# The first expert stage's opening slots moved into the drain of a lightning-attention stage, with routing in fewer slots

## The reference, cut to what matters

```
x = x + lightning_attention(layernorm(x))   # chunks of 128, 16 heads, a state carried from chunk to chunk
x = x + ffn(layernorm(x))                   # 32 experts of width 96, at most 7 of the top 8 in use per token
x = x + attention_b(layernorm(x))           # softmax attention with rotary positions
x = x + ffn(layernorm(x))                   # the same experts again

ffn:  probs = softmax(x @ gate_weight.T); top 8; keep those whose running share is under 0.8, plus one
      out  += (silu(g) * u) @ w_down.T * share        for each token and each expert kept for it
```

## Time and profile before

| | |
|---|---|
| median of 3 runs | 1141.58 us (1138.09 to 1143.42) |
| the profiled execution's own time | 1150.82 us |
| its span | 1149.0 us |
| PE busy | 893.2 us (78%) |
| POOL busy | 654.5 us (57%) |
| DVE busy | 586.1 us (51%) |
| ACT busy | 544.4 us (47%) |
| indirect DMAs issued by POOL | 288 results (995 ns each), 224 rows (1002 ns each) |
| mean granted TensorE clock | 0.894 |

### The profile page before, as it was taken

One profiled execution on the slowest core, in us unless ns is written; L12 is line 12 of the kernel. 1 busy time (PEld: TensorE's weight loads), 2 busy tenths in 40 slices (PEclk: granted clock), 3 DMA queues, 4 the chain that ended last, 5 costly groups with the idle time before them and its releaser, 6 DMA issues. The chain is left out here.

```text
span 1149.0 us, 20703 instructions
## 1 busy us (share of the span) xinstructions
PE 893.2 (78%) x5504; PEld 673.5 (59%) x5504; DVE 586.1 (51%) x2104; ACT 544.4 (47%) x1071; POOL 654.5 (57%) x652
## 2 busy tenths in 40 slices
PE   5999998852896699997338897988649877999940
PEld 4666665531785599996223453544228766999940
DVE  4566785845362122226846478664622711223565
ACT  5333456520463255654237767665515533555530
POOL 2576568776676777771541010474665567777760
PEclk9999999985798799999669898988878988999985
DMA  9900012122767777665230000125336587766976
GB/s 340 361 2 2 1 46 81 70 80 92 225 207 252 242 224 221 214 208 191 100 129 33 33 33 33 47 102 220 113 110 209 172 270 253 219 220 215 295 245 216
DMA packets 93231, 181.64 MB, mean 158 GB/s; under 512 B 18985, under 2 KB 73788, under 8 KB 92736
## 3 DMA queue, kind: packets, MB, share of 16 engines
q1 hardware_dynamic: 68544, 114.19, 31.1%
q0 software_dynamic: 24576, 66.13, 15.8%
HBM read 96.34 MB, written 92.27 MB: 164 GB/s over the span
## 5 line engine op out<-in xcount | busy, mean ns | idle before, releaser
L1295 POOL DMA_INDIRECT result_rows<-ys,result_slots x288 | 286.5, 995 | 105.5 <-issue 85.7
L981 POOL DMA_INDIRECT expert_rows<-route_rows,index x224 | 224.5, 1002 | 105.4 <-issue 91.0
L1944 ACT ACTIVATE b_probs<-ps 128x1024 f32<-128x1024 f32 x128 | 127.7, 1030 | 46.6 <-PE ps L1794 46.6
L1447 PE MATMUL ps<-w_gu,f_xts 128*128 x576 | 112.9, 341 | 3.1 <-issue 2.0
L1447 PE MATMUL ps<-w_gu,g_xts 128*128 x576 | 111.0, 337 | 3.8 <-ACT g_xts L1490 2.0
L1540 DVE SCALAR_TENSOR_TENSOR f_h<-ps,f_xs,f_gate 128x96 f32<-128x96 f32 x144 | 39.1, 313 | 121.0 <-ACT f_gate L1497 93.4
L1447 PEld LDWEIGHTS ps<-w_gu,f_xts 128*128 128x128 f32 x576 | 97.4, 199 | 5.6 <-issue 5.4
L1447 PEld LDWEIGHTS ps<-w_gu,g_xts 128*128 128x128 f32 x576 | 96.1, 197 | 6.2 <-issue 6.0
L1540 DVE SCALAR_TENSOR_TENSOR g_h<-ps,g_xs,g_gate 128x96 f32<-128x96 f32 x144 | 39.1, 313 | 115.2 <-ACT g_gate L1497 101.6
L1806 PE MATMUL ps<-b_probs,b_v_pad 128*32 128x512 f32 x512 | 78.3, 687 | 13.2 <-issue 6.9
L1508 ACT COPY ys<-ps 128x512 f32<-128x512 f32 x144 | 83.6, 581 | 1.8 <-PE ps L1466 1.8
(11 more groups left out here) (361 smaller groups left out, 1849.9 us busy)
## 6 DMA issues: line engine op xcount, KB each, us to landing
parts<-result_rows SPq DMA_DIRECT2D x32, 896.0 KB, 4.8
f_xs<-expert_rows SPq DMA_DIRECT2D x144, 160.0 KB
g_xs<-expert_rows SPq DMA_DIRECT2D x144, 160.0 KB
expert_rows<-pad_rows SPq DMA_DIRECT2D x64, 160.0 KB, 2.3
w_gu<-in_Wgu SPq DMA_DIRECT2D x1, 6144.0 KB, 17.5
expert_rows<-pad_rows SPq DMA_DIRECT2D x1, 5120.0 KB, 40.4
result_rows<-ys,result_slots POOLq DMA_INDIRECT x288, 3.4
f_w_d<-in_Wdown SPq DMA_DIRECT2D x1, 4096.0 KB, 29.8
```

Source lines behind the costliest of these rows:

```text
L981: self.nc.gpsimd.indirect_dma_start(xs, bass.IndirectOffsetOnAxis(self.index[:, f, t, r:r + 1].bitcast(U32), 0), self.x_rows(f)[:, t, :], ...
L1295: self.nc.gpsimd.indirect_dma_start(self.y_dram, bass.IndirectOffsetOnAxis(self.slots[:, i, j:j + 1].bitcast(U32), 0), self.ys[:, i, j, :] ...
L1447: ins = nc.tensor.matmul(ps[:, bank_gu[u % 2], j * GU:(j + 1) * GU], xts[:, u % 2, o:o + P], w_gu[:, k, bass.ds(experts[j] * GU, GU)], sta ...
L1944: nc.scalar.activation(probs[:, u % RING, :, :], ps[:, 2 * (u % 2):2 * (u % 2) + 2, :], ACT.Exp, scale=float(HD) ** -0.5).then_inc(exp_don ...
```

## The change

The experts are no longer a block of their own after lightning. `experts` becomes a set of generators, one for each engine, that yield after each slot. Lightning's block takes them as `then`: from unit 65 on (`THEN = DRAIN - THEN_SLOTS`) every drain unit ends with one slot of the experts on PE, ACT, POOL and DVE, so that slots 0 to 9 stand in units 65 to 74, and `run_all` appends the rest. SP starts them after its first loads and the last of lightning's projections. For the experts `g` after attention there is still a block of its own (`alone`). Their buffers (`Overlay`) lie over lightning buffers that are no longer read. In slots 0 to 9 of `f`, pairs have one PSUM bank for turned rows and one for gate and up in place of two (`Banks`), since the drain uses the others.

Routing's 15 steps stand in 11 slots (`TOGETHER`): 0 and 1 together, 3 (which is empty) left out, 9 with 11, 10 with 12. `PLACED` goes from 13 to 9, in lightning and in both expert stages. Batch 3's step 0 in `f` stands in slot 10. POOL's early result pairs, before batch 3's scatters, are 3 in place of 7 in both stages. A ring place of `xs` is given back at `h_ready`, when DVE has multiplied. The padding stores of `f` follow the load of pair 25 in one run; those of `g` start in slot 17; in both, four row numbers are loaded by one register load.

```
+THEN_SLOTS = 10
+    THEN = DRAIN - THEN_SLOTS
...
+            slots = then.tensor(pe)
             for u in range(UNITS, UNITS + DRAIN):
                 finish(u // QUADS, u % QUADS, B - 1)
                 route(UNITS * (B - 1) + u)
+                if u >= UNITS + THEN:
+                    advance(slots)
+            run_all(slots)
...
             first_loads(sp, 1)
+            sp.wait_ge(kv_sb, NT)
+            run_all(then.sync(sp))
...
-    STEPS = 15
-    PLACED = 13
+    TOGETHER = ((0, 1), (2,), (4,), (5,), (6,), (7,), (8,), (9, 11), (10, 12), (13,), (14,))
+    PLACED = len(TOGETHER) - 2
...
             if u >= RING:
-                sp.wait_ge(y_ready, u - RING + 1)
+                sp.wait_ge(h_ready, u - RING + 1)
...
-                if u >= 2:
-                    pe.wait_ge(h_ready, u - 1)
+            if banks.before(banks.gate_up, u) is not None:
+                pe.wait_ge(h_ready, banks.before(banks.gate_up, u) + 1)
...
+        def started(first, scattered):
+            return first + max((Routing.ALL - scattered) // 2, Routing.PLACED)
...
+        def results_at(u, first, scattered, last):
+            start = started(first, scattered)
+            early = first + max(6, (Routing.ALL - scattered) // 2)
+            pairs = TILES // 2 if last else TILES // 2 - LATER
+            if early <= u < start:
+                yield u - early
+            if u == start + Routing.ALL // 2:
+                for v in range(max(0, start - early), pairs):
                     yield v
+
+        def pads_at(u, last):
+            if last and 17 <= u < 17 + E // 4:
+                yield 4 * (u - 17)
+            if not last and u == (TILES - PHASES[-1][1]) // 2 - 1:
+                yield from range(0, E, 4)
...
+                first, scattered = (0, 18) if final else (THEN_SLOTS, 16)
+                split = Banks(0, 5, (), ((0, 2), (3, 4), (6, 7))) if final else Banks(
+                    THEN_SLOTS, 5, ((0,), (4,), (7, 6)), ((0, 2), (4, 3), (7, 6)))
```

More of the change, by code:

```diff
@@ L560, in _ @@
             batches(body)
+            slots = then.scalar(act)
             for u in range(UNITS, UNITS + DRAIN):
@@ new lines, in experts, with place, from_list @@
+    down_ready, y_ready, pads_stored = sem("down_ready"), sem("y_ready"), sem("pads_stored")
+    out_stored = sem("out_stored")
+    bank_h = banks.hidden
+    bank_route = [ps[:, 1, :]] * 4
+    starts = [sum(tiles for _, tiles in PHASES[:n]) // 2 for n in range(len(PHASES))]
+    assert place_at.at <= RESULTS_AT
+    def place(u):
+        n = max(n for n, start in enumerate(starts) if start <= u)
+        return n, u - starts[n]
+    def from_list(eng, engine, u, first, most):
+        n, at = place(u)
+        if at == 0:
+            routing.wait_tiles(eng, n)
+        return nc.values_load_multi_w_load_instructions(
+            routing.tab[at:at + 1, n, first:first + 2], engines=[engine], min_val=0, max_val=most,
+            skip_runtime_bounds_check_because="the list is clipped to the experts and their rows")[1]
@@ L1365, in from_list, with experts_of, rows_of, sync @@
+    def experts_of(eng, engine, u):
+        return from_list(eng, engine, u, 0, E - 1)
+    def rows_of(sp, u):
+        return from_list(sp, mybir.EngineType.SP, u, 2, STORED - P)
+    def sync(sp):
+        def load(u):
             n, at = place(u)
             if at == 0:
[L1367 to L1370, removed]
@@ new lines, in store_pads @@
+        def store_pads(first, count):
+            if first == 0:
+                routing.wait_tiles(sp, LAST)
+            rows = nc.values_load_multi_w_load_instructions(
+                routing.pads[0:1, first:first + count], engines=[mybir.EngineType.SP], min_val=0,
+                max_val=DUMMY - P, skip_runtime_bounds_check_because="an expert has at most every token")[1]
+            for row in rows:
+                sp.dma_start(xs_dram[bass.ds(row, P), :],
+                             routing.tables.pad_rows[:, :]).then_inc(pads_stored, 16)
@@ new lines, in gpsimd @@
+    def gpsimd(pool):
+        for u in range(PAIRS + FLUSH):
+            for step, f in steps_at(u):
+                routing.gpsimd(pool, step, f)
+            for f, k in scatters_at(u):
+                routing.scatter(pool, f, k, xs_dram)
+            for v in results_at(u):
+                pool.wait_ge(y_ready, v + 1)
+                results.scatter(pool, v)
+            yield
+        if out_rows is None:
+            results.wait_scattered(pool, PAIRS - LATER)
+    return Programs(sync, tensor, scalar, vector, gpsimd)
@@ L1378, in _, with alone @@
+def alone(nc, programs):
+    with nc.Block() as block:
         @block.sync
         def _(sp):
[L1380 to L1387, removed]
-                    sp.wait_ge(y_ready, u - RING + 1)
-                for j, row in enumerate(rows_of(sp, u)):
-                    sp.dma_start(xs[:, u % RING, j, :], xs_dram[bass.ds(row, P), :]).then_inc(loaded[u % RING], 16)
@@ L1392, in store_pads @@
[L1392 to L1396, removed]
-                                         max_val=DUMMY - P,
-                                         skip_runtime_bounds_check_because="an expert has at most every token")
-                    sp.dma_start(xs_dram[bass.ds(row, P), :],
-                                 routing.tables.pad_rows[:, :]).then_inc(pads_stored, 16)
```

475 lines of the change are left out of this document (249 added, 226 removed).

## The result

| | before | after |
|---|---|---|
| median | 1142.99 us (1138.09 to 1151.07, 11 runs) | 1157.91 us (1152.78 to 1161.59, 11 runs) |
| profiled execution, span | 1149.0 us | 1153.6 us |
| batch 3's step 0 in `f` | 287.82 | 310.48 |
| batch 3's row numbers in `f` | 335.00 | 365.72 |
| pair 26 of `f` turned | 400.47 | 411.36 |

The ratio is 1.013 (95% interval 1.0105 to 1.0154): slower, where 1121 and faster were forecast, and outside the range of 1100 to 1136. The stage `f` lost 22.0 us (539.31 to 561.27), the rest of the program won.

A forecast was written before the change was run, and what follows sets the result against it. The drain had no full engine; PE bound `f` later, with POOL's backlog only a tenth faster and becoming the bound. `f` wins 7.1 and `g` 13.7, so 1141.6 - 20.8 = 1121 us, range 1100 to 1136.

The forecast's parts named there:

- Batch 3's routing: In `f`, first product to row numbers: 36.5 us less three slots (8.6) gives 27.9; row numbers at 336.1, against 335.18.
- The half of 15.8: Start of `f`'s first pair: placing batches 0 and 1 four units earlier wins 7.9 us, with ends 0 and 15.8.
- The tenth product: In the drain: nine more pairs take 25.7 us plus 5.8 not hidden, so it is at 306.9, with step 0 behind it.
- The half of 11.6: In the drain: DVE's chunk ends and steps 13 and 14 add 5.8 us not hidden, with ends 0 and 11.6.
- The backlog and the end of the block: POOL in `f`: 116 scatters take 148.5 us, then 3.4 to land and 1.3; attention starts at 532.2, 7.1 won.
- Pair 26 turned: PE in `f`: pair 26 turns at 385.8, not 400.47, 14.7 us earlier, so POOL becomes the bound.
- In g: Expert stage after attention: row numbers 11.4 us earlier, 138 scatters at 1.304 each, tile 14 read at 1119.5; 13.7 won.
- Hidden pairs: Rival, drain: X completes at about 288, step 0 at about 290, 17 us ahead of 306.9; time 1104; chance 0.18.
- Pair 26 no earlier: Rival, `f`: padding stores still last 49.8 us, pair 26 stays at about 400, `f` wins nothing; time 1128; chance 0.12.
- Turns of waiting: Rival, drain: PE, ACT and DVE go in turn, nine pairs take 52.1 us, not 31.5; time 1141; chance 0.07.
- Half clock: Rival, drain: PE at half speed, nine pairs at 6.6 us take 59.4, `f` loses 20.8; time 1149; chance 0.08.
- Port shut: Rival, drain: POOL shut out whenever DVE works, up to 35 us more, row numbers slip 24; time 1144; chance 0.03.

## Why the prediction was wrong

**The step that failed** is "*Batch 3's routing*. From the first product to the row numbers it was 36.5 ... With steps put together it has three slots fewer: 27.9". It took a stretch of the kernel before and shortened it, as if the stretch took its surroundings along. Before, the slots of routing lay over pairs 0 to 12, and all but the last of these read rows scattered by 270. Ten slots later they lie over pairs 10 to 18, and pair 12 needs the batch whose scatters stand behind routing's own power. From step 0 at 310.48 to the row numbers it was 55.2 us. The sum has 1.3 + 27.9 = 29.2 for it. The text never named the two waits that make most of the difference: PE's for pair 12 (20.73), ahead of batch 3's turns, and POOL's power (10.26), which makes PE's longer (9.58 without it). The order of the program, shown ahead of the prediction, had the second of them in its POOL piece: the power ahead of the last 12 scatters.

The stall is not all of the 26.0 between them. Without PE's wait at pair 12 the stretch is 55.2 - 20.73 = 34.5, and with five slots 36.0 - 3.81 = 32.2; both are above 29.2. The forecast had taken its stretch from the first product and put it behind step 0. But before, the first product ended 10.9 behind the start of step 0 (298.73 and 287.82), with the power long done. Now the power and all steps after it are still to come when the tenth product ends. That this is the rest of the gap is read from the two orders; no run tests it alone.

**The terms around it held.** Pair 0 was forecast at 268.8 and turned at 271.65. The half of 15.8 taken for routing four units earlier was too much: batch 1's row numbers came at 213.90, 1.9 earlier than the earlier trace rows, not 7.9. The tenth product was forecast at 306.9 and ended at 310.5, so ten pairs in the drain cost what was said. The half of 11.6 for steps not hidden was a guess that came out near, and it hides that pair 0 was 2.9 later than forecast. From row numbers to the backlog 42.9 was forecast and 407.51 - 365.90 = 41.6 measured. The backlog and the end of the block took 148.5 + 4.7 by forecast, and 561.27 - 407.51 = 153.8. The padding stores in one run took 23.3, forecast 26.5. Pair 26 turned 25.6 later than forecast (411.36 for 385.8), where the row numbers were 29.8 late. With row numbers done at 365.90 in place of 336.1, the prediction's own sum gives 532.2 + 29.8 = 562.0 for attention's start, measured 561.27. POOL set the end of `f`, as forecast.

**A reading that was wrong.** "The block starts only when X is complete" and "X completes at about 288" do not fit the rows: X was complete at 281.18, and the block's end waited for the drain's scatters (theory D). The forecast's sum does not rest on it. It counts where the block still ends there, as in the kernels with a block of their own.

**In g** the forecast held against the block's own start (SP's first load, 858.43 before and 876.25 after). Timelines of POOL and SP after, which answer to the earlier trace rows:

```profile
957.17 0.97 POOL L1318 DMA_INDIRECT result_rows<-ys,result_slots  x1 [3.33 <-issue]
...
1134.86 1.28 POOL L1318 DMA_INDIRECT result_rows<-ys,result_slots  x1 [0.30 <-issue]
```
```profile
876.25 46.46 SPq L1449 DMA_DIRECT2D g_xs<-expert_rows  x36
...
1138.98 0.32 SPq L1327 DMA_DIRECT2D parts<-result_rows  x1
```

The backlog starts 80.9 after the block's start, before 89.0: 8.1 won, forecast 11.4. Its 138 scatters go at 1.297 each, forecast 1.304. Tile 14 is read 262.7 after the start, before 274.8: 12.1 won, forecast 13.7. POOL's last scatter starts at 1134.86 and lands, with 3.3 from issue to landing, at about 1138.2, just ahead of tile 14's read. The place in SBUF that tile 14 needs comes free when DVE has added tile 12. In the kernel before that is at 1132.70, and the read follows 0.5 later (1133.21). With the change it is at 1135.79, and the read follows only 3.2 later. So POOL's last scatter now sets tile 14, as the forecast had it. DVE's timelines, before and after:

```profile
1132.70 0.42 DVE L1315 TENSOR_TENSOR X<-X,parts 128x256 f32<-128x256 f32 x1
```
```profile
1135.79 0.42 DVE L1338 TENSOR_TENSOR X<-X,parts 128x256 f32<-128x256 f32 x1
```

In medians less is seen. `f` lost 22.0 and the time grew by 14.9, which leaves 7.1 for all behind it, where the two profiles show 17.4. The profiled execution of before was 1150.82, 7.8 above its median, and that of after 1155.39, 2.5 below; together they are the 10.3 between. Some of it lies in attention, which took 319.1 in the profile of before and 315.0 in that of after, and 313.5 to 317.4 in the six other undisturbed profiles. Where the rest lies is open.

**The rivals.** Hidden pairs (1104): no, since X's last piece came at 304.76. Pair 26 no earlier because of the stores: they were faster than that. Turns of waiting: no, the ten products came at a spacing of 3.6, close to the forecast's 3.5 and not 5.8. Half clock, the slower rival, named the right sign (1149) with the wrong mechanism: from 271 to 310 the granted clock was 0.87, and of the first four pairs two ran slowly, all later ones up to the tenth near 1.5 for the eight matmuls. In PE's timeline of the changed kernel:

```profile
274.44 2.92 PE L1506 MATMUL ps<-w_gu,f_xts 128*128 x8
278.67 1.56 PE L1506 MATMUL ps<-w_gu,f_xts 128*128 x8 [0.45 <-DVE f_h L1599]
284.17 2.65 PE L1506 MATMUL ps<-w_gu,f_xts 128*128 x8 [3.28 <-DVE f_h L1599]
289.92 1.56 PE L1506 MATMUL ps<-w_gu,f_xts 128*128 x8 [0.28 <-DVE f_h L1599]
```

Port shut: no (its own sum gives 1145, where 1144 is written). From 240 to 302 POOL's scatters averaged 1008 ns beside a busier DVE (35.2 of 62 us, before 27.3), in POOL's groups of that stretch:

```profile
L1004 POOL DMA_INDIRECT expert_rows<-route_rows,index x31 | 31.2, 1008 | 16.0 <-issue 16.0
```

None of the cases was the one that came. None of them asked what the moved chain of 11 dependent steps would stand behind.

## What to carry to other kernels

When steps are moved by whole slots, each slot has new neighbours: for each engine, list what the moved step now stands behind, and ask when that item's data is ready. A stretch's duration can only be carried over if its neighbours wait for nothing new. Overlap is worth what the hole holds and no more: kernels with five slots in the drain are 1.4 to 1.9% faster than before, and ten, which delayed the producer that everything later needs, lost 1.3%. Most of that gain is not the overlap's. A block of its own with the rest of the change, and ten scatters in the drain, took 1130.81 us; in the same job five slots with six early pairs took 1121.58 and the kernel before 1143.46. So overlap and early pairs together gave 9.2 us, and 12.7 of the 21.9 came without any pair in the drain.

## What had not been expected of the hardware

The same program differs far more from job to job than between its versions. In three jobs the kernel before took 1142.99 to 1143.46 us, in five others 1302 to 1321 us. Whether this goes by chip is not shown: chip number 0 stands for one job of each kind. The first 290 us are the same: with five slots a product of DVE starts at 287.60 in the one and at 287.59 in the other. After that all stages are longer. For five slots with six early pairs, `f` ends at 610.79 in place of 527.74, attention takes 350.8 in place of 314.0, and `g` to the end 356.7 in place of 277.6. In `f`, PE's weight loads, DVE and ACT stop now and then for up to 15 us without a releaser that the profile names ("issue" and "remote" name no engine), while POOL's longest wait of that kind in the same stretch is 2.7. Waits of 400 to 500 in the first disturbed run of that kernel:

```profile
DVE f_h L1599 <- issue: 36.4, 9, 14.8
PEld ps L1517 <- issue: 23.6, 6, 10.4
ACT f_gate L1556 <- remote: 22.0, 8, 7.3
POOL result_rows L1318 <- issue: 21.9, 51, 2.7
```

What stops them is not shown. But it changes verdicts: five slots had 0.9858 in one job and 1.0063 in another, and in the disturbed jobs every version of the change that ran was slower than the kernel before.
